# Two small transfers move from ScalarE's queue to SyncE's, and a bias addition moves from GpSimd to VectorE

## The reference, cut to what matters

```python
q = x @ Wq.T + bq;  k = context @ Wk.T + bk;  v = context @ Wv.T + bv
scores = jnp.einsum('bhtd,bhcd->bhtc', q, k) / jnp.sqrt(d)
attn = jax.nn.softmax(scores, axis=-1)
out = jnp.einsum('bhtc,bhcd->bhtd', attn, v)   # then @ Wo + bo
x = x + tanh(g_xattn) * out
```

## Time and profile before

| | |
|---|---|
| median of three runs | 3847.09 us |
| the profiled execution's own time | 3839.65 us |
| its span, first to last instruction | 3838.5 us |
| mean granted TensorE clock | 0.94 |
| PE busy | 3406.2 us (89%) |
| DVE busy | 2159.3 us (56%) |
| ACT busy | 2035.6 us (53%) |
| POOL busy | 681.8 us (18%) |
| the chain that ended last, by engine | PE 66%, DVE 12%, DMA 9% |

### The profile page before, as it was taken

How to read it: one execution, slowest core, us unless ns; L and a number is a source line. 1 busy time by engine, 2 the same in 40 slices (tenths; PEclk the granted TensorE clock), 3 DMA queues, 4 the chain that set the end, 5 groups by cost and what they waited for, 6 DMA issues and landing times.

```text
span 3838.5 us, 52360 instructions
## 1 busy us (share of the span) xinstructions
PE 3406.2 (89%) x18396; PEld 1776.1 (46%) x18396; DVE 2159.3 (56%) x3519; ACT 2035.6 (53%) x4490; POOL 681.8 (18%) x712
## 2 busy tenths in 40 slices
PE   5999999978688989997899799989987979987997
PEld 2333333325432323332597322323326956687996
DVE  6767676736857777873402477767743033264333
ACT  2566666663236666775333266667772322254664
POOL 2211111001135341000312141210002010022332
PEclk8999999998879999999899799999997989998998
DMA  8132324105565343211864655644207521042554
GB/s 193 44 101 65 102 59 107 26 23 183 163 186 127 94 113 80 49 26 42 270 226 158 185 150 121 170 111 106 73 10 283 187 78 69 1 142 91 183 187 168
DMA packets 314685, 456.01 MB, mean 119 GB/s; under 512 B 66315, under 2 KB 234195, under 8 KB 312251
## 3 DMA queue, kind: packets, MB, share of 16 engines
q1 hardware_dynamic: 233206, 285.70, 27.2%
q0 software_dynamic: 29568, 104.65, 8.1%
q10 hardware_dynamic: 51653, 62.32, 5.8%
HBM read 292.46 MB, written 153.91 MB: 116 GB/s over the span
## 4 chain that ended last, share of the span: by engine, by line
PE 66%; DVE 12%; DMA 9%; issue 4%; ACT 4%; POOL 4%; SPq 2%; ACTq 0%; another core or an unknown queue 0%; POOLq 0%; DVEq 0%
PE pv L1325 14%; PE m L1289 11%; PE s L1311 9%; DVE mxp L1172 9%; PE h L2808 5%; PE y L2816 5%; PE h L2382 4%; PE y L2391 4%; PE y L1791 2%; PE s L1771 2%; DMA sums<-rc 2%; PE s L1256 2%; ACT e_t L1403 1%; DMA ot<-sums 1%; PE m L1333 1%
## 5 line engine op out<-in xcount | busy, mean ns | idle before, releaser
L1172 DVE TENSOR_REDUCE mxp<-m 128x1 f32<-128x802 f32 x1536 | 1447.9, 987 | 525.5 <-PE m L1289 521.6
L1403 ACT ACTIVATE e_t<-s 128x512 f32<-128x512 f32 (+1 forms) x2496 | 1340.5, 599 | 553.5 <-PE s L1311 534.4
L1289 PE MATMUL m<-kaug,qaug 97*128 97x401 bf16 x3072 | 812.1, 347 | 101.8 <-DVE mxp L1172 55.5
L1311 PE MATMUL s<-qaug,kaug 100*128 100x512 bf16 (+1 forms) x2496 | 859.4, 386 | 33.7 <-ACT e_t L1403 28.6
L1325 PE MATMUL pv<-e_t,v 128*32 128x512 f32 (+1 forms) x4992 | 669.7, 609 | 0.2
L1311 PEld LDWEIGHTS s<-qaug,kaug 100*128 100x128 bf16 (+1 forms) x2496 | 229.4, 99 | 733.0 <-ACT e_t L1403 518.6
L1289 PEld LDWEIGHTS m<-kaug,qaug 97*128 97x128 bf16 x3072 | 273.7, 100 | 511.2 <-DVE mxp L1172 269.2
L127 POOL TENSOR_TENSOR rstd<-rstd,mhalf 128x16 f32<-128x16 f32 (+2 forms) x9 | 24.2, 2690 | 1192.9 <-DVE rstd L120 1192.9
L2878 ACT ACTIVATE ez<-h,b 128x128 f32<-128x128 f32 x440 | 120.1, 389 | 158.0 <-PE h L2808 157.9
L1325 PEld LDWEIGHTS pv<-e_t,v 128*32 128x32 f32 (+1 forms) x4992 | 98.6, 108 | 214.2 <-ACT e_t L1403 160.3
L2269 DVE SCALAR_TENSOR_TENSOR y<-y,b 128x256 f32<-128x256 f32 x39 | 16.6, 425 | 304.8 <-PE y L2391 304.8
(11 more groups left out here) (370 smaller groups left out, 3561.3 us busy)
## 6 DMA issues: line engine op xcount, KB each, us to landing
w<-in_L_w POOLq DMA_DIRECT2D x78, 1024.0 KB, 5.4
w<-in_L_w SPq DMA_DIRECT2D x24, 1024.0 KB, 12.8
xregion<-zero ACTq DMA_DIRECT2D x10, 2056.0 KB, 12.1
kaug<-kparts SPq DMA_DIRECT2D x16, 1200.8 KB
kaug<-kready SPq DMA_DIRECT2D x32, 600.4 KB
kaug<-kready SPq DMA_DIRECT2D x16, 1200.8 KB
vn<-values SPq DMA_DIRECT2D x8, 1536.0 KB
values<-p_vb ACTq DMA_DIRECT2D x21, 512.0 KB
```

Source lines behind the costliest of these rows:

```text
L1172: dve.tensor_reduce(a.mxp[:, u.g % 2, half, n:n + 1], a.m_slot[u.m % 2][:].rearrange("p (a n) -> p a n", a=2)[:, :, 0:PIECE + 1], AX.XY, A ...
L1289: m = pe.matmul(slot[:, 512 * k:512 * k + PIECE + 1], a.qaug[0:R_MAX, u.g, j, P * qc:P * qc + P], a.kaug[0:R_MAX, u.g, j, k0:k0 + PIECE + ...
L1311: pe.matmul(slot[0:KW[u.k], :], a.kaug[0:R_ALL, u.g, u.j, P * u.k:P * u.k + KW[u.k]], a.qaug[0:R_ALL, u.g, u.j, :], start=True, stop=True) ...
L1403: act.activation(a.e_t[0:KW[u.k], e % 2, u.j, :], a.s_slot[u.s % 3][0:KW[u.k], :], ACT.Exp).then_inc(s_free.sem, 1)
```

## The change: what it does

1. `low` and `spread` become one unit, `spread`, on SP's queue: SP waits for the reciprocals and for all five loads of the group, issues `sums<-rc`, waits for its landing, and issues `ot<-sums`. ACT issues neither.
2. One semaphore, `moved`, counts all seven transfers of a group. DVE's reciprocal now waits for the load of `rc` and the four moves, where it waited for the load of `rc`.
3. `NORM_STEPS` goes from 6 to 5.
4. POOL's additions of `bob` go. DVE adds `bob` to a tile behind each `out`, after a wait for its own x + gate * product.
5. `b_made` is split into two semaphores, and `tables` of the first layer is called `ident`.

```diff
-NORM_STEPS = 6
+NORM_STEPS = 5
+
+MOVES = 1 + HG + 2
...
     def normalise(self, g, b):
 
-        for kind in ("sum", "rec", "low", "spread"):
+        for kind in ("sum", "rec", "spread"):
             self.add(kind, b=b, g=g)
             yield
...
+def head_spread_sp(kn, a, u):
+
+    sp, r_full, moved = kn.nc.sync, kn.sema("r_full"), kn.sema("moved", DMA)
+    sums = kn.dram["sums"]
+    sp.wait_ge(r_full.sem, r_full.at(u.n + 1))
+    sp.wait_ge(moved.sem, moved.at(MOVES * u.n + 1 + HG))
+    sp.dma_start(sums.rearrange("j (a c) -> (j a) c", a=P // HG), a.rc[:]).then_inc(moved.sem, DMA)
+    sp.wait_ge(moved.sem, moved.at(MOVES * u.n + 2 + HG))
+    lo = HG * HD * (u.g % 2)
+    sp.dma_start(a.rs[lo:lo + HG * HD, u.g // 2, :],
+                 sums.rearrange("j (a n) -> j a n", a=1).to_broadcast([HG, HD, T])).then_inc(moved.sem, DMA)
...
-            pool.wait_ge(b_made.sem, b_made.at(3))
-            for b in range(B):
-                xb = kn.x[:, TT * b:TT * b + TT, :]
-                pool.tensor_tensor(xb, xb, a.bob[:].rearrange("p (t n) -> p t n", t=1).to_broadcast([P, TT, D]),
-                                   ALU.add).then_inc(biased.sem, 1)
...
         elif u.kind == "rec":
-            dve.wait_ge(summed.sem, summed.at(3 * u.n + 1))
+            dve.wait_ge(moved.sem, moved.at(MOVES * u.n + 1 + HG))
             dve.reciprocal(a.rc[:], a.rc[:]).then_inc(r_full.sem, 1)
         elif u.kind == "norm":
-            dve.wait_ge(moved.sem, moved.at(HG * 2 * (u.n + 1)))
-            dve.wait_ge(summed.sem, summed.at(3 * 2 * (u.n + 1)))
+            dve.wait_ge(moved.sem, moved.at(MOVES * 2 * (u.n + 1)))
...
         elif u.kind == "out":
             xt = x[:, u.b * TT + u.k, :]
-            if u.k == 0:
-                dve.wait_ge(biased.sem, biased.at(u.b + 1))
             dve.wait_ge(m_full.sem, m_full.at(u.m + 1))
             dve.scalar_tensor_tensor(xt, a.m_slot[u.m % 2][:, 0:D], a.gate, xt, ALU.mult, ALU.add).then_inc(m_free.sem, 1)
+            dve.wait_ge(m_free.sem, m_free.at(u.m + 1))
+            i = dve.tensor_tensor(xt, xt, a.bob[:], ALU.add)
+    i.then_inc(x_done.sem, 1)
...
-        elif u.kind == "low":
-            head_low_act(kn, a, u)
-        elif u.kind == "spread":
-            head_spread_act(kn, a, u)
```

More of the change, by code:

```diff
@@ L495, in add @@
             u.m = self.next("m")
-        if kind in ("pv", "turn", "sum", "rec", "low", "spread", "norm", "take", "peak"):
+        if kind in ("pv", "turn", "sum", "rec", "spread", "norm", "take", "peak"):
             u.n = self.next(kind)
@@ L776, in head_attention @@
             sig(name, DMA).close(n)
-        sig("moved", DMA).close(HG * NG * B)
-        sig("summed", DMA).close(3 * NG * B)
-        ends = ["m_free", "s_free", "z_full", "r_full", "td", "moved", "summed"]
+        sig("moved", DMA).close(MOVES * NG * B)
+        ends = ["x_done", "s_free", "z_full", "r_full", "td", "moved"]
         if not ready:
@@ L890, in head_sp @@
             head_sum_sp(kn, a, u)
+        elif u.kind == "spread":
+            head_spread_sp(kn, a, u)
         elif u.kind == "turn":
@@ L898, in head_sum_sp @@
 def head_sum_sp(kn, a, u):
-    sp, z_full, m_full = kn.nc.sync, kn.sema("z_full"), kn.sema("m_full")
-    moved, summed = kn.sema("moved", DMA), kn.sema("summed", DMA)
+    sp, z_full, m_full, moved = kn.nc.sync, kn.sema("z_full"), kn.sema("m_full"), kn.sema("moved", DMA)
     sp.wait_ge(z_full.sem, z_full.at(u.n + 1))
     if u.n:
-        sp.wait_ge(moved.sem, moved.at(HG * u.n))
-        sp.wait_ge(summed.sem, summed.at(3 * u.n))
+        sp.wait_ge(moved.sem, moved.at(MOVES * u.n))
     if u.b:
@@ L913, in head_sum_sp @@
             sp.wait_ge(kept.sem, kept.at(a.p.stores[f]))
-    sp.dma_start(a.rc[:], a.z[HD::P // HG, :]).then_inc(summed.sem, DMA)
+    sp.dma_start(a.rc[:], a.z[HD::P // HG, :]).then_inc(moved.sem, DMA)
     for j in range(HG):
@@ L1130, in head_dve @@
     turns = units("turn")
-    ot_full, moved, summed, biased = kn.sema("ot_full"), kn.sema("moved", DMA), kn.sema("summed", DMA), kn.sema("biased")
+    ot_full, moved = kn.sema("ot_full"), kn.sema("moved", DMA)
     ld_q = kn.sema("ld_q", DMA)
@@ L1227, in head_pe @@
     if not a.ready:
-        ident = kn.sema("tables", DMA)
+        ident = kn.sema("ident", DMA)
         pe.wait_ge(ident.sem, ident.at(1))
@@ L1339, in head_act @@
     s_full, s_free, m_free, pv_done = (kn.sema(n) for n in ("s_full", "s_free", "m_free", "pv_done"))
-    z_full, v_taken, b_made, filled = (kn.sema(n) for n in ("z_full", "v_taken", "b_made", "filled"))
+    z_full, v_taken, b_scaled, filled = (kn.sema(n) for n in ("z_full", "v_taken", "b_scaled", "filled"))
     ld_k = kn.sema("ld_k", DMA)
     rope = a.rope is not None
-    moved, summed = kn.sema("moved", DMA), kn.sema("summed", DMA)
+    moved = kn.sema("moved", DMA)
     if not a.ready:
@@ L2936, in setup_dve @@
     dve, cst = kn.nc.vector, kn.cst
-    ident, ready = kn.sema("tables", DMA), kn.sema("set")
+    ident, ready = kn.sema("ident", DMA), kn.sema("set")
     dve.memset(cst["ones"][:], 1.0)
```

42 lines of the change are left out of this document (15 added, 27 removed).

## The result

The changed kernel takes 3866.73 us (median of five, 3862.93 to 3868.33), the kernel before 3841.43 us (median of five, 3839.39 to 3850.54): ratio 1.0059, 95% interval 1.0047 to 1.0070, or 22.7 us more (18 to 27). The ratio is taken from more executions than the five of each median, which lie 25.3 us apart. The profiled execution was a long one: 3879.41 us, span 3878.2. One execution of the kernel of experiment 4 took 12554.3 us, and its ratio leaves that one out.

A forecast was written before the change was run, and what follows sets the result against it. PE and DVE, alternating, were taken to bound the kernel. Gains of -22 and costs of +9, +4, +4.5, +8 and +6 sum to +9.5, from the median 3847.1 forecast as 3857 us; overall range 3838 to 3882.

The forecast's parts named there:

- the rival with all additions on the path: Rival, chance 0.19: DVE's additions of bob all delay the kernel, 22 us instead of 6, giving 3873.
- ACT's waits, -12: Third layer: ACT no longer waits for sums<-rc behind a 2 MB clear, 8 groups at 1.5 us each, -12.
- `norm` after the third layer's second batch, -8: In that passage sums<-rc and ot<-sums land earlier, so DVE is at 2571 where it was at 2579.3, -8.
- (a): Tails of three layers: reciprocal starts 2.5 us later, waiting for the moves, plus 0.4 for an addition; 3 x 2.9 = +9.
- (b): Four places, one in the second layer, others in the first: already late reciprocals wait for the moves, 4 x 1 = +4.
- (c): Passage after second layer's first batch: late sums<-rc holds norm, +15.5; the group behind loses a stall, -11; left +4.5.
- (d): Passage after third layer's first batch: sums<-rc issued behind a kf load slowed by the clear, norm later, about +8.
- (e): 36 additions of bob on DVE inside passages, 0.4 us each, under half counted: +6, bounds 0 and 14.
- the prediction's second sign: The prediction is wrong if DVE's idle time behind out doesn't shrink by the additions.
- The queue as no obstacle: Rival, chance 0.18: sums<-rc passes stores and loads ahead on SP's queue, landing 2 us after issue; sum -10, 3837.
- The stall of (c) not given back: Rival, chance 0.17: SP is late again behind the second layer's first passage, the 8.40 us stay, +11, 3868.
- SP late everywhere: Rival, chance 0.04: SP 4 us late in each of the 10 groups with key loads, +40 on the sum, 3895.

The follow-up runs named there:

- experiment 4: Changed kernel with one step more for the work of a passage, 5 steps elsewhere: ratio 1.0008 to the kernel before, 9 us below the changed kernel.
- experiment 2: Kernel before with only the additions of bob moved from GpSimd to VectorE behind each out: ratio 1.0012 to the kernel before, +4.6 us.
- experiment 5: Changed kernel with NORM_STEPS 6 instead of 5 everywhere: ratio 1.0068 to the kernel before, +26 us.
- Experiment 9: Changed kernel with the clear of a batch's fourth take issued with the first take's instead: 3861.19 us in one execution.
- experiment 6: Kernel before with one edit, the reciprocal also waiting for the four moves of its group: ratio 1.0045 to the kernel before, +17.3 us.
- experiment 8: Kernel before with SP issuing sums<-rc and ot<-sums for each batch's first three groups, nothing else changed: ratio 0.9941, 22.8 us below the kernel before.

## Why the prediction was right, and where not

The range held the time (3866.73 in 3838 to 3882), and slower was forecast with 0.55. The step was forecast at +9.5 us and is +22.7, and on another chip +12.3. That the range held is luck in part: its upper end came from the rival with all additions on the path, which experiment 2 puts out, and the terms missed by up to 10 us each, some upwards and some downwards. By its own steps:

- **ACT's waits, -12: right**, -11.8 in the profile that it was read from. That it is a number of one chip was not seen: the earlier trace rows show a transfer waiting for a 2 MB clear, and ACT's waits for it add up to 16 us in one execution and 26 in another. The rule that the prediction cites beside it would have `sums<-rc` freed from the clear on SP's queue, and that is not what happened: it still takes 9.1 to 10.3 us there. The gain comes from ACT no longer standing in the wait.
- **`norm` after the third layer's second batch, -8: wrong, +1.8.** The issue came as forecast (one store ahead, 12.9 us after the copy). The failing step is the price of the two transfers, 3 and 4.5 us beside the clear; they took 5.9 and 10.9. The rule cited from the Trainium skill ("DMA: Bandwidth & Descriptors", queues, rings and completion order) has them in another ring than the clear; by its own round robin it doesn't free them from sharing the DMA engines with it, and that half of it was not put into the price. That ACT no longer waits is no test of the rule, since ACT issues neither of them now; the 9.1 to 10.3 us of `sums<-rc` on SP's queue show no gain from the separate ring when the clear was issued 1.0 us before, and experiment 5 shows 1.4 to 1.9 us when it was issued 0.5 us after. Experiment 9 shows the clear as the cause: without it in the passage `norm`'s wait is 0. The earlier trace rows had a warning: `ot<-sums` took 15.7 us there, behind the clear in ACT's own queue.
- **(a) Tails, 2.5 us each: nearly right**, 2.6 at the reciprocal and 2.2 at `norm`, of which experiment 6 shows 7 us on the path.
- **(b) Late reciprocals, +4: the mechanism right, the sum wrong.** Without the edit of NORM_STEPS the wait costs 3.5 us at each of three places, not 1.8 (experiment 6). With it the prediction left about 1 us at each; measured is nothing, 59.7 us in the changed kernel for 60.1 to 60.9 before.
- **(c) Passage after the second layer's first batch, +4.5: right in place and kind, too small.** `sums<-rc` was issued behind the stores and loads named, 30.1 us after the copy (forecast 32.1), `ot<-sums` landed after 37.0 (forecast 39.2). The cost was 17.8 (forecast 15.5), though DVE's wait was only 14.2. The windows over the stall (columns: from and to, the length, busy us of PE, PEld, DVE, ACT and POOL, clock, DMA share, GB/s) show one reason:

```profile
1329.00:1339.00 10.00, 5.26 (x31) 1.35 (x29) 2.69 (x3) 4.53 (x9) 9.53 (x9) 1.00 0.45 144
1339.00:1349.00 10.00, 0.91 (x3) 0.29 (x4) 2.51 (x4) 0.00 (x0) 9.53 (x9) 0.50 0.73 209
1349.00:1359.00 10.00, 9.70 (x43) 4.28 (x43) 7.33 (x11) 4.15 (x8) 6.57 (x7) 0.82 0.56 162
```

  TensorE idles, its granted clock falls to the lower level of 1.2 GHz, and the stretch behind runs at 0.82 of the full one. What that cost was not measured by itself. (c)'s other half gave back less than forecast: the 8.40 us wait of the reciprocal is gone, but the group takes 6.3 us less, not 11. It was never going to reach 39.0; POOL works beside it, before the change as well, and DVE's small operations on two SBUF operands take 0.97 us instead of 0.17, with the shift's product waiting for them:

```profile
1401.08 0.97 DVE L1192 TENSOR_TENSOR mx<-mxp 128x16 f32<-128x16 f32 x1
1402.09 0.17 DVE L1193 TENSOR_SCALAR nm<-mx 128x16 bf16<-128x16 f32 x1
1402.30 1.01 DVE L1194 SCALAR_TENSOR_TENSOR mx<-mx,nm 128x16 f32<-128x16 f32 x1
...
1445.04 0.17 DVE L1192 TENSOR_TENSOR mx<-mxp 128x16 f32<-128x16 f32 x1
```

  GpSimd's row beside the first of them:

```profile
1400.99 1.04 POOL L1070 TENSOR_TENSOR ks<-kf,ones 128x512 bf16<-128x512 f32 x1
```

- **(d) Third layer's first passage, +8: right**, +8.5 and +6.2; `sums<-rc` issued 21.3 us after the copy, as forecast, and `norm` waits 14.2 us where it waited 7.1.
- **(e) The additions, +6 and 1 in the tails: right**, +4.6 (1 to 9) in experiment 2. The rival that had them all on the path (22 us) is out. DVE's idle time at the `out`s shrank by 4.5 us in experiment 2 and 5.5 in the changed kernel, for 48 additions of 24.1 and 21.2 us, so the prediction's second sign is met in direction, and where the rest of them is hidden was not found.
- **The other rivals.** The queue as no obstacle: so it was in (c), where `sums<-rc` landed 2.7 us after its issue, but there the late issue decides; in (d) it took 8.3 us. In the first layer, directly behind SP's loads of keys, it took 14.2 to 14.8. The stall of (c) not given back: in part. SP late everywhere: out, by experiment 8; its time of 3895 was a slip, for 3857 and 40 are 3897.
- **Not priced: where NORM_STEPS puts the `out`s.** It was read as "`norm` two maxima earlier" only. The units of a passage are given out by NORM_STEPS + 5, so all four `out`s moved against the maxima, and their products wait 30 times instead of 5: 9 us by experiment 4. The rows of the order shown ahead of the prediction have it: in the changed order four maxima stand between `norm` and the first `out`, where there were three. From the two traces alone the additions seemed to be what pays these 1.0 to 2.4 us a passage; experiment 2 told otherwise.

So the loss is the two late passages (+20 with the stall given back), the tails (+7), the bunched `out`s (+9) and the additions (+5, by experiment 2), against the third layer's waits (-12 or more); the last two costs lie partly inside the passages, and the terms, which add up to 29 us, overlap by some of it. Against the forecast the sharing with the clear is 10 us off, the placing of the `out`s 9 and (c) 7, while (b) and (e) were some 7 too high; these overlap as well.

Left open: how the loss is spread over the feed-forward stretches, which differ by 8 us between executions of one kernel, and why the three late groups of experiment 6 lose 3.5 us for a wait that is 1.9 longer.

## What to carry to other kernels

Moving a small transfer to another queue frees the engine that waited in the old one, not the transfer: ask separately what is issued ahead of it in the new order, and what large transfer moves beside it. Whether it is issued just before or just after that large transfer can decide (1.8 against 9.1 us at one place here). Move only the instances that have nothing late ahead of them; here three groups in four gave 23 us, and the fourth, with its transfers late in SP's order, took most of that back. A constant that spreads work over steps moves everything that shares its generator, so the order is to be read for each of these operations.

## What the runs showed of the hardware

- Two small transfers of 8 KB and 128 KB took 5.9 and 10.9 us beside a 2 MB clear in another engine's queue, 2.1 and at most 4.3 us without it.
- The 8 KB transfer took 9.1 to 10.3 us when it was issued 1.0 us behind such a clear in another engine's queue, 8.3 to 9.0 when 3.5 us behind it in the same queue, and 1.4 to 1.9 when 0.5 us ahead of it in another.
- The second of two 2 MB clears issued one behind the other held ScalarE's queue for 2.2 us (2.77 for both), one alone 0.6.
- A VectorE operation of 128x16 on two SBUF operands took 0.97 us beside a GpSimd operation on SBUF, 0.17 without one.
- The kernel before took 3841 us on one chip and 3860 on another, and ACT's waits for a transfer behind the clears were 16.3 and 26.2 us in two profiles.
